# A two-layer network on one core: layer 0's attention hands ScalarE other tiles for its second squares, those of rows 4 to 6 of each head quad instead of rows 0 to 2

## The chip, the cores and the metric

The kernel runs on one core of a Trainium2 chip. Every time is device time in microseconds (us). The kernel before took 859.58 us as the median of 3 runs (859.4 to 862.9).

The engines carry these names in the profile: PE is TensorE's matmul part (PEld its weight load), DVE is VectorE, ACT is ScalarE, POOL is GpSimd. Each works through its own list of instructions strictly in order, and they meet at semaphores.

## The reference

Two layers, each an attention and a gated feed-forward part. The change is in layer 0's attention only: 1024 tokens, 16 heads of 16 channels, and a causal attention whose weights are not a softmax but the fourth power of the scores.

```python
def polynomial_attention(q, k, v, degree, is_causal):     # degree 4
    a = jnp.einsum('bhnd,bhmd->bhnm', q, k) ** degree
    if is_causal:
        a = jnp.tril(a)
    denom = jnp.sum(a, axis=-1, keepdims=True)
    return jnp.einsum('bhnm,bhmd->bhnd', a / denom, v)
...
xn = _layernorm(x)
s = _L0_attn_ref(xn, ...)            # changed stage
g = _silu(_L0_ffn_ref(xn, ...))
x = x + s * g                        # then layer 1
```

## The kernel before

Layer 0's attention stands between layer 0's feed-forward part and layer 1, and nothing of either runs beside it but a few small pieces. The 16 heads are worked in four **groups** of four heads. Inside a group a **row** is one block of 128 keys: row j (0 to 7) holds the scores of the keys 128j to 128j+127, on the partitions, against all queries from 128j on, so rows grow shorter, from 1024 queries down to 128. Rows are numbered through, R = 0 to 31, and R % 8 is j.

A row is cut into **units**, one PSUM bank pair each. In rows 0 to 3 a unit is two heads by half of the row's queries (four units per row); in rows 4 and 5 two heads by all queries (two units); rows 6 and 7 are one unit of four heads. That makes 22 units per group and 88 in all, of 1024, 896, 768, 640 or 512 elements per partition. Units 0 to 21 are the first group, 22 to 43 the second, 44 to 65 the third, 66 to 87 the fourth. In the second group units 22 to 25 are row 0, 26 to 29 row 1, 30 to 33 row 2, 34 to 37 row 3, 38 and 39 row 4, 40 and 41 row 5, 42 row 6, 43 row 7.

A unit goes through these steps:

- **scores** (PE, L595): the matmuls into one of three PSUM pairs. A pair is used again only when the first square of the unit that had it three steps earlier is done.
- **first square** (ACT, L1079): from PSUM into SBUF. Always ScalarE's.
- **second square** (in place in SBUF): on DVE (L1402, a tensor_tensor that multiplies the tile with itself) or, for units in ON_ACT0, on ACT (L1082). ScalarE takes the second square of unit n-1 after the first square of unit n.
- **mask** (POOL, L1772): an affine_select that zeroes the 128-wide diagonal block, only of the units that begin at a row's first query (u[2] == 0). 14 of a group's 22 units have one.
- **out** (PE, L613): the row's tile as the moving operand against the values, into two PSUM banks, one per half of the queries, when every second square and mask of the row is done.

Finished rows lie in a ring of four slots. Two of the slots reuse other tiles, so the trace calls row 0, 1, 4 and 5 of a group A, rows 2 and 6 qk_tok, and rows 3 and 7 stack. PE's order is a list worked out ahead (order0): a row's out comes behind the scores of the fourth unit after its last, one half at a time, with scores of the next unit between the halves. So out of row 2 of the second group stands just ahead of scores of unit 38.

At a group's end ACT copies the summed output out of PSUM (L1053, o_raw), PE transposes it (L624), and DVE divides (L1383 and L1385), which frees the PSUM pair of that transpose. The copy stands in ACT's list before the first square of the next group's unit 4, the division in DVE's list behind its unit 6. In the third group PE also transposes the divided output of the first two groups (L633), ACT rounds it (L1059, xT_hi) and DVE takes the rest (L1392, xT_lo), behind unit 55 in DVE's list.

Of the kernel before, what the change touches and what calls it, by code (L numbers as in the profile page):

```python
# [18 lines left out]
NT = TOK // P  # L19
# [16 lines left out]
def units0(j):  # L36

    w = (NT - j) * P
    size = 2 if j < 6 else 4
    cuts = [(0, w // 2), (w // 2, w)] if j < 4 else [(0, w)]  # L40
    return [(list(range(i, i + size)), a, e) for i in range(0, QUAD, size) for a, e in cuts]


UNITS0 = [(R, *unit) for R in range(ROWS0) for unit in units0(R % NT)]
DONE0 = [sum(1 for u in UNITS0 if u[0] <= R) for R in range(ROWS0)]
ON_ACT0 = [u[2] > 0 and u[1][0] == 2 and u[0] % NT < 3 for u in UNITS0]
BY_ACT0 = [sum(ON_ACT0[:n + 1]) for n in range(len(UNITS0))]
BY_DVE0 = [n + 1 - BY_ACT0[n] for n in range(len(UNITS0))]
MASKED0 = [sum(1 for u in UNITS0 if u[0] <= R and u[2] == 0) for R in range(ROWS0)]
# [105 lines left out]
def build_program(nc, x_in, wqkv_in, wout_in, lns_in, lnb_in, packed_in, scales_in,  # L155
# [5 lines left out]
    with ExitStack() as ctx:  # L161
        def sem(name):
            return ctx.enter_context(nc.semaphore(name))
# [94 lines left out]
        def A0_unit(n):  # L258

            R, heads, a, e = UNITS0[n]  # L260
            return A0_row(R)[:, heads[0]:heads[-1] + 1, a:e]
# [90 lines left out]
        def rows_of(b):  # L352
# [32 lines left out]
        s0_ps, s0_sq, s0_four, s0_four_act, s0_mask = (sem("s0_ps"), sem("s0_sq"), sem("s0_four"), sem("s0_four_act"),  # L385
                                               sem("s0_mask"))
# [126 lines left out]
        def _(pe):  # L513
# [300 lines left out]
            def logits(_, half):  # L814

                pe.wait_ge(rw_ready, 1)
                o = side_slot()
                tk = slice(half * HALF, (half + 1) * HALF)
                for c in range(NC):
                    last = mm3(o[0:NE, :], rw_hi[:, c], rw_lo[:, c], xT_hi[:, c, tk], xT_lo[:, c, tk], c == 0, c == NC - 1)  # L820
                last.then_inc(lgT_ps, 1)

            def turn_logits(*_):
                pe.wait_ge(lgT_copied, 2)
                o = side_slot()
                for t in range(NT):
                    last = pe.transpose(o[:, t * NE:(t + 1) * NE], lgT[:, t * P:(t + 1) * P], ident[0:NE, 0:NE])
                last.then_inc(lg_ps, 1)

            def ranks(*_):  # L830

                pe.wait_ge(mask_ready, 2)
                pe.wait_ge(rk_ready, 1)
                o = side_slot()
                chosen = r_m.rearrange("p t e -> p (t e)")
                pe.matmul(o[:, 0:NT * NE], before[:], chosen, start=True, stop=False)
                for t in range(1, NT):
                    pe.matmul(o[:, t * NE:NT * NE], ones[:], chosen[:, 0:(NT - t) * NE], start=False, stop=(t == NT - 1))
                for t in range(NT):
                    last = pe.matmul(o[:, NT * NE:(NT + 1) * NE], ones[:], r_m[:, t, :], start=(t == 0), stop=(t == NT - 1))  # L840
                last.then_inc(rk_ps, 1)
# [106 lines left out]
        def _(act):  # L948
# [115 lines left out]
            for n in range(len(UNITS0)):  # L1064
# [14 lines left out]
                act.activation(dst, src, ACT.Square).then_inc(s0_sq, 1)  # L1079
                if n >= 1 and ON_ACT0[n - 1]:  # L1080
                    act.wait_ge(s0_sq, n)
# [123 lines left out]
        def _(dve):  # L1205
# [191 lines left out]
            for n in range(len(UNITS0)):  # L1397
                R, heads = UNITS0[n][0:2]
                if not ON_ACT0[n]:
                    dve.wait_ge(s0_sq, n + 1)  # L1400
# [284 lines left out]
        def _(pool):  # L1685
# [81 lines left out]
            for n in range(len(UNITS0)):  # L1767
                if UNITS0[n][2]:
                    continue
                diag = A0_unit(n)[:, :, 0:P]  # L1770
                pool.wait_ge(s0_four, BY_DVE0[n])
                pool.affine_select(out=diag, in_=diag, compare_op=ALU.is_ge, fill=0.0, base=0,  # L1772
                                   pattern=[[0, len(UNITS0[n][1])], [1, P]], channel_multiplier=-1).then_inc(s0_mask, 1)
            def split_wqk(n):
# [251 lines left out]
```

## Time and profile before

| what | value |
|---|---|
| median of 3 runs | 859.58 us (859.4 to 862.9) |
| the profiled execution's own time | 856.94 us |
| its span, first to last instruction | 855.2 us |
| PE, DVE, ACT, POOL busy over the span | 92%, 71%, 54%, 50% |
| layer 0's attention, first square to last copy's start | 200.22 to 298.93 us of the span |
| in 199 to 300 us: PE, DVE, ACT, POOL busy | 78.8, 86.7, 84.8, 48.0 of 101 us |

The profiled execution is 2.6 us shorter than the median of the runs, so sums made in the trace are compared with 856.94 us and the difference is then added to 859.58. In the stage of the change no engine is busy throughout: what counts there is who waits for whom.

### The profile page before, as it was taken

What the parts mean: (1) busy time and instruction counts of PE and PEld (TensorE: products, weight loads), DVE (VectorE), ACT (ScalarE), POOL (GpSimd) and SP (SyncE); (2) the same over time, 40 slices, a digit from 0 to 9 for tenths busy, and PEclk for the clock granted to TensorE, in tenths of its full rate; (3) what the DMA queues carried; (4) which work ended last, traced back from release to release, by engine and by line L of the source; (5) the groups of instructions that cost most, each with busy time, mean ns of one, the idle gap of its engine ahead of it and who ended that gap; (6) DMA issues with size and microseconds to landing.
All of it is one profiled execution on the core that took longest, in us unless ns stands there. A gap on an engine that the chain in (4) does not pass through costs nothing.

```text
span 855.2 us, 13950 instructions
## 1 busy us (share of the span) xinstructions
PE 783.4 (92%) x4871; PEld 639.4 (75%) x4871; DVE 611.4 (71%) x1077; ACT 465.4 (54%) x822; POOL 423.7 (50%) x479
## 2 busy tenths in 40 slices
PE   6999999978777878898999999999999999999996
PEld 5776776754222367687988889989999999998884
DVE  8588868557998767888967886766767654445555
ACT  4433342279888733676645556565656555655431
POOL 1767837333555445445434447568663412665540
PEclk9999999998999989999999999999999999999999
DMA  5211194000000041000000001111110569643107
GB/s 182 75 38 37 38 292 135 1 1 1 1 1 1 1 126 30 22 7 11 21 8 13 8 25 57 38 38 49 47 44 1 207 126 351 214 149 106 51 5 243
DMA packets 50116, 59.82 MB, mean 70 GB/s; under 512 B 13559, under 2 KB 41084, under 8 KB 50048
## 3 DMA queue, kind: packets, MB, share of 16 engines
q1 hardware_dynamic: 45488, 50.49, 19.4%
q0 software_dynamic: 4560, 8.44, 2.8%
q8 instruction: 41, 0.67, 0.3%
q14 instruction: 27, 0.22, 0.1%
HBM read 41.11 MB, written 21.86 MB: 74 GB/s over the span
## 4 chain that ended last, share of the span: by engine, by line
PE 56%; DVE 12%; ACT 6%; POOL 6%; issue 5%; DMA 1%; POOLq 0%; ACTq 0%; DVEq 0%; SPq 0%
PE ps L786 12%; PE ps L516 8%; PE ps L518 8%; PE ps L517 8%; PE ps L879 4%; PE ps L876 3%; PE ps L910 3%; DVE cap L1477 2%; POOL A L1772 2%; DVE swap L1467 2%; PE ps L858 2%; PE ps L698 2%; PE ps L558 2%; PE ps L613 1%; PE ps L795 1%
## 5 line engine op out<-in xcount | busy, mean ns | idle before, releaser
L1131 ACT ACTIVATE cap<-cap 128x1024 f32<-128x1024 f32 (+7 forms) x128 | 87.1, 680 | 123.1 <-DVE cap L1477 123.0
L786 PE MATMUL ps<-V,P 128*128 128x129 f32 x1152 | 152.7, 279 | 0.0
L786 PEld LDWEIGHTS ps<-V,P 128*128 128x128 f32 x1152 | 145.3, 194 | 2.7
L1477 DVE SCALAR_TENSOR_TENSOR cap<-dist,ps 128x1024 f32<-128x1024 f32 (+7 forms) x128 | 95.1, 750 | 27.1 <-PE ps L518 22.1
L1696 POOL TENSOR_SCALAR_AFFINE_SELECT P<-P 128x128 f32<-128x128 f32 x128 | 38.8, 303 | 148.6 <-ACT P L1136 148.3
L1828 POOL DMA_INDIRECT y_scratch<-y_sb,aux_s x63 | 62.1, 985 | 61.2 <-ACT y_sb L1176 39.3
L1136 ACT ACTIVATE P<-cap 128x1024 f32<-128x1024 f32 (+7 forms) x128 | 87.6, 685 | 4.1
L516 PE MATMUL ps<-q_hi,k_hi 128*128 128x512 f32 x192 | 72.2, 376 | 7.9 <-DVE cap L1477 6.3
L518 PE MATMUL ps<-q_lo,k_hi 128*128 128x512 f32 x192 | 66.9, 349 | 0.0
L517 PE MATMUL ps<-q_hi,k_lo 128*128 128x512 f32 x192 | 66.8, 348 | 0.0
L1803 POOL TENSOR_TENSOR rot<-rot,swap 128x512 f32<-128x512 f32 x40 | 52.2, 1306 | 14.4 <-DVE swap L1467 14.2
L516 PE MATMUL ps<-xT_hi,w_hi 128*128 128x512 f32 x128 | 56.4, 441 | 2.9 <-POOL w_lo L1716 1.8
L1016 ACT ACTIVATE e_g<-ps 128x512 f32<-128x512 f32 x32 | 19.1, 598 | 68.5 <-PE ps L518 68.5
L1624 DVE TENSOR_SCALAR gu<-ps 128x256 f32<-128x256 f32 (+1 forms) x63 | 28.9, 459 | 38.0 <-PE ps L879 15.8
L1467 DVE TENSOR_TENSOR swap<-ps,sin 64x512 f32<-64x512 f32 x80 | 55.1, 688 | 1.1
L1402 DVE TENSOR_TENSOR A<-A 128x1024 f32<-128x1024 f32 (+2 forms) x40 | 49.6, 1287 | 4.4 <-ACT A L1079 4.4
L518 PE MATMUL ps<-xT_lo,w_hi 128*128 128x512 f32 x128 | 50.6, 396 | 0.0
L517 PE MATMUL ps<-xT_hi,w_lo 128*128 128x512 f32 x128 | 50.5, 394 | 0.0
L1168 ACT ACTIVATE sg<-gu 128x128 f32<-128x128 f32 (+1 forms) x63 | 20.4, 323 | 50.5 <-DVE gu L1624 50.5
L1079 ACT ACTIVATE A<-ps 128x1024 f32<-128x1024 f32 (+2 forms) x48 | 43.4, 965 | 7.7 <-PE ps L595 7.7
L595 PEld LDWEIGHTS ps<-QT,KT 64*128 64x128 f32 x192 | 16.4, 190 | 41.6 <-ACT A L1079 19.3
L516 PEld LDWEIGHTS ps<-q_hi,k_hi 128*128 128x128 f32 x192 | 36.6, 190 | 14.0 <-DVE cap L1477 7.8
(288 smaller groups left out, 2111.6 us busy)
## 6 DMA issues: line engine op xcount, KB each, us to landing
xg_scratch<-blank SPq DMA_DIRECT2D x1, 8127.0 KB, 31.2
xa<-xg_scratch SPq DMA_DIRECT2D x63, 128.0 KB, 2.3
ew<-in_experts SPq DMA_DIRECT2D x3, 1920.0 KB, 7.9
y<-y_scratch SPq DMA_DIRECT2D x8, 512.0 KB, 5.0
pk<-in_packed SPq DMA_DIRECT2D x8, 384.0 KB, 3.2
pks<-in_scales SPq DMA_DIRECT2D x8, 384.0 KB, 4.3
ew<-in_experts SPq DMA_DIRECT2D x1, 3072.0 KB, 11.2
wqk<-in_wqk SPq DMA_DIRECT2D x20, 128.0 KB, 2.0
```

The source lines that it names most:

```text
L516: pe.matmul(o, l_hi, r_hi, start=start, stop=False)
L517: pe.matmul(o, l_lo, r_hi, start=False, stop=False)
L518: return pe.matmul(o, l_hi, r_lo, start=False, stop=stop)
L786: last = pe.matmul(ps[:, 4 + r % 2, o:o + D1 + 1], P1[:, h % 2, a:a + P], V1[:, j, h // REP, :], start=(j == 0), stop=(j == t))
L1079: act.activation(dst, src, ACT.Square).then_inc(s0_sq, 1)
L1131: act.activation(cap[:, n % 2, 0:w], cap[:, n % 2, 0:w], ACT.Tanh, scale=1.0 / (CAP * float(D1) ** 0.5))\
L1136: act.activation(P1[:, h % 2, OFF[j]:OFF[j] + w], cap[:, n % 2, 0:w], ACT.Exp, scale=CAP)\
L1402: dve.tensor_tensor(a, a, a, ALU.mult).then_inc(s0_four, 1)
L1467: last = dve.tensor_tensor(swap[to, i % 2, :], b[frm, :], sin1[frm, tk], ALU.mult)
L1477: dve.scalar_tensor_tensor(out=cap[:, n % 2, 0:w], in0=dist[:, 0:w], scalar=slope, in1=psf[:, 1024 * (n % 2):1024 * (n % 2) + w], op0=ALU. ...
L1803: pool.tensor_tensor(r, r, swap[:, i % 2, :], ALU.add).then_inc(pj_rot, 1)
L1828: pool.indirect_dma_start(out=y_dram, out_offset=bass.IndirectOffsetOnAxis(ap=aux_s[:, b, 0:1].bitcast(U32), axis=0), in_=y_sb[:, b % YRIN ...
```

## The change

ON_ACT0, the list of units whose second square is ScalarE's, is another one. Before it held, in each group, the second head pair's second half of rows 0, 1 and 2 (units 3, 7 and 11 of the group; 1024, 896 and 768 elements; none of them masked). Now it holds the second head pair of rows 4 and 5 and the one unit of row 6 (units 17, 19 and 20 of the group; 1024, 768 and 1024 elements; all of them masked). So both before and after 3 of 22 squares per group are ScalarE's, and DVE has 19. The masks of the three units now wait for ScalarE's semaphore.

```diff
-ON_ACT0 = [u[2] > 0 and u[1][0] == 2 and u[0] % NT < 3 for u in UNITS0]
+ON_ACT0 = [(u[0] % NT in (4, 5) and u[1][0] == 2) or u[0] % NT == 6 for u in UNITS0]
 BY_ACT0 = [sum(ON_ACT0[:n + 1]) for n in range(len(UNITS0))]
 BY_DVE0 = [n + 1 - BY_ACT0[n] for n in range(len(UNITS0))]
...
                 diag = A0_unit(n)[:, :, 0:P]
-                pool.wait_ge(s0_four, BY_DVE0[n])
+                if ON_ACT0[n]:
+                    pool.wait_ge(s0_four_act, BY_ACT0[n])
+                else:
+                    pool.wait_ge(s0_four, BY_DVE0[n])
```

ACT's list before, from the first square of the second group's unit 26 on (the copy of the first group's output stands just ahead of it); 128x2x448 is a unit of row 1, 128x2x384 one of row 2 or row 5, by its tile:

```order
L1079 ACTIVATE A<-ps 128x2x448
L1082 ACTIVATE A<-A 128x2x512
L1079 ACTIVATE A<-ps 128x2x448 x3
L1079 ACTIVATE qk_tok<-ps 128x2x384
L1082 ACTIVATE A<-A 128x2x448
L1079 ACTIVATE qk_tok<-ps 128x2x384 x3
L1079 ACTIVATE stack<-ps 128x2x320
L1082 ACTIVATE qk_tok<-qk_tok 128x2x384
L1079 ACTIVATE stack<-ps 128x2x320 x3
L1079 ACTIVATE A<-ps 128x2x512 x2
L1079 ACTIVATE A<-ps 128x2x384 x2
L1079 ACTIVATE qk_tok<-ps 128x4x256
```

The same stretch of ACT's list after the change:

```order
L1079 ACTIVATE A<-ps 128x2x448 x4
L1079 ACTIVATE qk_tok<-ps 128x2x384 x4
L1079 ACTIVATE stack<-ps 128x2x320 x4
L1079 ACTIVATE A<-ps 128x2x512 x2
L1079 ACTIVATE A<-ps 128x2x384
L1082 ACTIVATE A<-A 128x2x512
L1079 ACTIVATE A<-ps 128x2x384
L1079 ACTIVATE qk_tok<-ps 128x4x256
L1082 ACTIVATE A<-A 128x2x384
L1079 ACTIVATE stack<-ps 128x4x128
L1082 ACTIVATE qk_tok<-qk_tok 128x4x256
L1079 ACTIVATE A<-ps 128x2x512 x4
```

The three second squares have left the first squares of rows 0 to 3 and stand among those of rows 4 to 7, all three ahead of the next group's first squares.

DVE's list before, from row 4 of the first group to row 3 of the second:

```order
L1402 TENSOR_TENSOR A<-A 128x2x512 x2
L1402 TENSOR_TENSOR A<-A 128x2x384 x2
L1402 TENSOR_TENSOR qk_tok<-qk_tok 128x4x256
L1402 TENSOR_TENSOR stack<-stack 128x4x128
L1402 TENSOR_TENSOR A<-A 128x2x512 x3
L1402 TENSOR_TENSOR A<-A 128x2x448 x3
L1383 RECIPROCAL o_rden<-ps 128x32
L1385 TENSOR_TENSOR xa<-ps,o_rden 128x8x64
L1402 TENSOR_TENSOR qk_tok<-qk_tok 128x2x384 x3
L1402 TENSOR_TENSOR stack<-stack 128x2x320 x4
```

And after:

```order
L1402 TENSOR_TENSOR A<-A 128x2x512
L1402 TENSOR_TENSOR A<-A 128x2x384
L1402 TENSOR_TENSOR stack<-stack 128x4x128
L1402 TENSOR_TENSOR A<-A 128x2x512 x4
L1402 TENSOR_TENSOR A<-A 128x2x448 x3
L1383 RECIPROCAL o_rden<-ps 128x32
L1385 TENSOR_TENSOR xa<-ps,o_rden 128x8x64
L1402 TENSOR_TENSOR A<-A 128x2x448
L1402 TENSOR_TENSOR qk_tok<-qk_tok 128x2x384 x4
L1402 TENSOR_TENSOR stack<-stack 128x2x320 x4
```

Three squares have left rows 4 to 6, and rows 0, 1 and 2 have four each instead of three; that of row 1 stands behind the division.

## Rows read from the trace of the kernel before

**Rows 1.** The page's first line.
```profile
span 855.2 us, 13950 instructions
```

**Rows 2.** Windows between chosen first squares: units 22, 44, 66, 83, last copy.
```profile
core 0: us, PE busy (x) PEld busy (x) DVE busy (x) ACT busy (x) POOL busy (x), PEclk, DMA share, GB/s
222.81:246.15 23.34, 18.28 (x154) 6.82 (x152) 21.49 (x22) 20.71 (x27) 12.17 (x15) 1.00 0.01 1
246.15:271.91 25.76, 20.73 (x162) 7.81 (x160) 22.63 (x24) 21.89 (x29) 12.16 (x15) 0.93 0.00 1
271.91:290.15 18.24, 15.43 (x116) 6.04 (x114) 15.79 (x17) 16.87 (x22) 7.51 (x11) 0.91 0.00 1
290.15:298.93 8.78, 5.74 (x60) 1.87 (x58) 7.07 (x7) 3.83 (x6) 7.01 (x7) 1.00 0.00 0
```

**Rows 3.** Timeline of ACT: start, length, line, tile, count, wait before.
```profile
228.65 1.07 ACT L1082 ACTIVATE A<-A 128x1024 f32<-128x1024 f32 x1
229.60 2.54 ACT L1079 ACTIVATE A<-ps 128x896 f32<-128x896 f32 x3
...
236.86 0.87 ACT L1082 ACTIVATE qk_tok<-qk_tok 128x768 f32<-128x768 f32 x1
...
240.35 1.02 ACT L1079 ACTIVATE A<-ps 128x1024 f32<-128x1024 f32 x1
241.28 1.51 ACT L1079 ACTIVATE A<-ps 128x768 f32<-128x768 f32 x2
...
246.15 1.94 ACT L1079 ACTIVATE A<-ps 128x1024 f32<-128x1024 f32 x2 [1.96 <-PE ps L595]
```

**Rows 4.** Timeline of DVE, first two groups.
```profile
201.38 3.70 DVE L1402 TENSOR_TENSOR A<-A 128x1024 f32<-128x1024 f32 x3 [1.92 <-ACT A L1079]
205.00 0.68 DVE L1407 TENSOR_TENSOR wout_lo<-wout,wout_hi 128x512 fp32r<-128x512 f32 x1
...
230.56 2.09 DVE L1402 TENSOR_TENSOR A<-A 128x896 f32<-128x896 f32 x2 [0.56 <-ACT A L1079]
232.57 0.35 DVE L1383 RECIPROCAL o_rden<-ps 128x32 f32<-128x32 f32 x1
232.96 0.69 DVE L1385 TENSOR_TENSOR xa<-ps,o_rden 128x512 f32<-128x512 f32 x1
...
235.03 1.83 DVE L1402 TENSOR_TENSOR qk_tok<-qk_tok 128x768 f32<-128x768 f32 x2 [0.52 <-ACT qk_tok L1079]
...
240.56 4.71 DVE L1402 TENSOR_TENSOR A<-A 128x1024 f32<-128x1024 f32 x4
...
246.54 0.89 DVE L1402 TENSOR_TENSOR stack<-stack 128x512 f32<-128x512 f32 x1
```

**Rows 5.** Timeline of POOL: the masks.
```profile
234.58 0.41 POOL L1772 TENSOR_SCALAR_AFFINE_SELECT qk_tok<-qk_tok 128x256 f32<-128x256 f32 x1 [1.45 <-DVE qk_tok L1402]
...
242.06 4.83 POOL L1772 TENSOR_SCALAR_AFFINE_SELECT A<-A 128x256 f32<-128x256 f32 x4 [1.14 <-DVE A L1402]
...
297.67 0.63 POOL L1772 TENSOR_SCALAR_AFFINE_SELECT stack<-stack 128x512 f32<-128x512 f32 x1
```

**Rows 6.** Timeline of PE: row passes, and scores of unit 57.
```profile
214.49 0.42 PE L613 MATMUL ps<-qk_tok,V 128*32 128x256 f32 x4 [0.36 <-ACT qk_tok L1082]
...
237.82 0.64 PE L613 MATMUL ps<-qk_tok,V 128*32 128x256 f32 x8 [0.36 <-ACT qk_tok L1082]
...
244.61 1.07 PE L613 MATMUL ps<-A,V 128*32 128x512 f32 x8 [1.31 <-POOL A L1772]
...
254.36 1.93 PE L613 MATMUL ps<-A,V 128*32 128x512 f32 x8
...
262.91 0.41 PE L595 MATMUL ps<-QT,KT 64*128 64x320 f32 x2 [0.59 <-DVE xT_lo L1392]
```

**Rows 7.** One line's own summary: shortest, median, longest in ns.
```profile
L1392 DVE TENSOR_TENSOR xT_lo<-ps,xT_hi x4: 681/691/692, 261.6 to 304.9; 128x512 fp32r<-128x512 f32 x4
```

**Rows 8.** Waits in 199 to 300 us: total, times, longest.
```profile
PE ps L613 <- POOL A L1772: 8.7, 8, 1.4
```

## The prediction

> **What bounds the kernel now.** I read the windows first, then the timeline of each engine in the second group, the one group in which TensorE had its full clock throughout. The span is 855.2 us of an execution that took 856.94 [rows 1]. The windows run from the first square of unit 22 to that of unit 44 (the second group, 23.34 us), on to unit 66 (25.76), to unit 83 (18.24) and to the last copy (8.78) [rows 2]. In the second group ACT is busy 20.71 us and DVE 21.49 of 23.34: neither is full, so the order of waits sets the time, and I follow it in two parts.
>
> The **head** is rows 0 to 3, up to the first square of unit 39. There ACT has first and second squares in one queue, and PE's pass over row 2 (L613, 237.82) waits 0.36 us for ACT's second square of unit 33, which ends at 236.86 + 0.87 = 237.73 [rows 3, 6]. So ACT bounds the head. In the **tail**, rows 4 to 7, DVE runs four squares from 240.56 on without a gap, and the masks queue behind them: four masks take 4.83 us, where one alone takes 0.41 [rows 4, 5]. PE waits 1.31 us for a mask at 244.61, the scores behind that pass come late, and ACT sits idle 1.96 us before 246.15 [rows 3, 6]. The tail is bound by DVE and masks, the head by ACT. The change moves ACT's help from the one to the other; what it brings is what the tail can still use, less what the head now lacks.
>
> **What one square costs.** On DVE, call a the start-to-start time of a 1024 square, and m what a mask adds that slips in between two squares. The three from 201.38 to 205.00 hold one mask: 3a + m = 3.62. Those from 240.56 to 245.20 (4.71 long, less the 0.08 by which a 3.70 row outlasts its 3.62) are two of 1024 and two of 768 with three masks, 4.64. A 768 square is (1.83 - 0.07) / 2 = 0.88, an 896 square (232.57 - 230.56) / 2 = 1.005 [rows 4]. So 2a + 3m = 2.88, which gives a = 1.14, m = 0.20. A mask that waits is done 0.35 us after the next square has started: the four end at 246.89, and the square started at 246.54 [rows 4, 5]. The division is 0.99 (232.57 to 233.65, less the overlap).
>
> Behind that stands a rule: the Trainium skill, SBUF — State Buffer, section "SBUF: two separate sides", says that VectorE and GpSimd share one pair of SBUF ports as an exclusive lock, held for a whole instruction, against a VectorE operation with two SBUF inputs. The masks agree: 0.41 alone, some 1.2 beside back-to-back squares. By the rule alone, squares on ScalarE free the masks, and the change would be a gain; that is a rival below.
>
> On ACT a second square of 1024 is 0.95 (228.65 to 229.60), 0.12 less than its length, so one of 768 is 0.87 - 0.12 = 0.75. A first square is (1.94 - 0.10) / 2 = 0.92 for 1024 and (1.51 - 0.10) / 2 = 0.70 for 768, so about 0.48 for 512 [rows 3].
>
> **The tail after the change.** From the first square of unit 39, ACT's list holds 39, 40, second 39, 41, 42, second 41, 43, second 42, and then unit 44: 0.92 + 0.70 + 0.95 + 0.70 + 0.92 + 0.75 + 0.48 + 0.95 = 6.37 us. Before it was 246.15 - 240.35 = 5.80 with the idle time in it [rows 3]. ACT has no gap there any more: the idle 1.96 us are filled with 2.65 us of squares, and unit 44 comes 0.57 later. The passes over rows 4 to 7 wait for ACT's squares instead of masks and stay ahead of it. DVE, freed of 1.14 + 0.88 + 1.14 + 0.60 for masks, is idle before unit 44, which gains nothing, since its work comes from ACT.
>
> **The head after the change.** Now DVE has four squares of each of rows 0, 1 and 2. It can't start them before ACT has made the first one, so I count from ACT's first square of unit 44. That one is done 1.02 later; but ACT's second square of unit 42 ends 0.12 after unit 44's first square starts, so the masks of 42 and 43 run from 0.17 on, 0.63 each with DVE idle [rows 5], and DVE starts behind them at 1.43. Then 4 x 1.14 + 4 x 1.005 + 4 x 0.88 + 0.99 for the division = 13.09, and four masks slip in (rows 0, 0, 1 and 2; the others fall in gaps or the division), 0.80: the square of unit 55 ends at 15.32. The mask of unit 54 ends 0.35 behind and PE starts 0.10 after it: 15.77. Before, the same pass came at 237.82 - 222.81 = 15.01 [rows 2, 6]. The head becomes DVE's, 0.76 longer. From that pass to the first square of the next row 4's second unit it is 240.35 - 237.82 = 2.53 both times.
>
> What is queued behind this pass: scores of unit 38 and on (PE is in order), so all of ACT's tail. The two parts don't overlap, for each begins with what the other ends with.
>
> **The sum.**
> - Second group: 0.76 + 0.57 = +1.33.
> - First group: no lead. 201.38 + 4 x 1.14 + 0.61 (L1407) + 4 x 1.005 + 4 x 0.88 = 214.09, with five masks 215.09, and + 0.45 = 215.54, against 214.49 [rows 4, 6]: +1.05, and +0.57 for its tail: +1.62.
> - Third group: DVE ends unit 55 at 15.32, then two of L1392 at 0.69 [rows 7] = 16.70, when scores of unit 57 may start; before they started at 262.91 - 246.15 = 16.76, after the same instruction [rows 6]. Head -0.06, tail +0.57: +0.51.
> - Fourth group: 15.77 + 2.53 = 18.30 against 18.24 [rows 2]: +0.06. This and the third group lost time before to the half clock (granted 0.93 and 0.91): eight matmuls took 1.93 us at 254.36 and 1.07 at 244.61 [rows 2, 6]. It fell early in the head, where the new head has slack on PE. At the very end no group follows: ACT's last second square ends 6.37 + 0.12 later, two masks alone 1.26 + 0.05, then 0.63 to the copy as before (298.93 - 298.30): 8.43 against 8.78: -0.35. Together -0.29.
>
> Sum +1.33 + 1.62 + 0.51 - 0.29 = **+3.2 us**: 856.94 becomes 860.1 in the profiled execution, and the median 859.58 becomes **862.8**. Nothing else is priced: PE's instructions stay, the masks' other semaphore costs a wait on either engine, 0 by its kind; the work behind the stage waits for its end and shifts whole.
>
> **The rivals.**
> - *The head keeps up.* The mask costs and the late start are the least sure terms. Without them DVE's chain ends at 1.06 + 13.09 + 0.45 = 14.6, under 15.01, and only the tail's 0.57 stays: 3 x 0.57 + 0.05 - 0.35 = +1.4, 861.0. For it: masks are not always in the way; against it: DVE would be full 13 us on end. 17%.
> - *Masks are freed (faster).* PE waited 8.7 us in the stage for masks of tile A [rows 8]. If these waits go and the next rows come earlier by as much: 859.6 - 8.7 = 850.9. It decides if ACT's tail comes out under 5.80 us and the head doesn't wait for DVE. Against it: 6.37 of instructions stand in ACT's list, and nothing can go round it. 15%. The rule of the Trainium skill's page SBUF — State Buffer, told above, speaks for this one.
> - *Half clock in the wrong place (slower).* PE now waits longer in the head, right before the pass over row 2 and the stretch of 2.53 us in which PE is the chain. If the clock falls to half there, a pass costs 1.93 for 1.07 and the smaller one and the scores some 0.35 more, 1.2 a group: in three groups +3.6, 866.4. For it: two of the three windows before had such a stretch. 18%.
> - Forecast as summed: 50%, its own range 860.5 to 866.
>
> **How the numbers follow.** No change within 0.5% (4.3 us) is about what a measurement of this kernel can't tell from nothing. The forecast lies at +3.2, inside it for 33 of its 50 points and over it for 17; with the head that keeps up 17 more, so 33 + 17 = 0.50 for the same. Slower: 17 + 18 = 0.35. Faster 0.15. Range: the upper end takes in the half clock, 868; the lower stops short of freed masks, but takes in a half of their gain against the head's loss, 857. Outside lie some 10% below and 8% above.
>
> **What would show it.** Right: DVE squares of rows 0 to 2 in an unbroken run of about 13 us in each group, PE's pass over row 2 waiting for DVE or its mask at about 15.8 us after the first square of the group; ACT with gaps in the head and none in the tail; masks of rows 4 to 6 at 0.4 to 0.8 instead of 1.1; from unit 22 to 44 some 24.7 us. Wrong: ACT still idle before unit 44, or that window under 23.3; or a stage of equal length with the difference elsewhere; or a granted clock in the stage far under 0.93.

## The result, and the profile after

The changed kernel took 862.07 us (median of 20 runs, 858.73 to 868.38), the kernel before 859.49 beside it: ratio 1.0033, 95% interval 1.0017 to 1.0049, so 1.5 to 4.2 us slower, 2.8 in the middle (the medians differ by 2.6). The predicted 862.8 was 3.2 over the 859.58 of before.

The windows of the changed kernel, cut at the same squares as [rows 2] (first squares of units 22, 44, 66, 83 and the last copy):

```profile
core 0: us, PE busy (x) PEld busy (x) DVE busy (x) ACT busy (x) POOL busy (x), PEclk, DMA share, GB/s
223.53:248.00 24.47, 19.88 (x156) 7.08 (x152) 20.43 (x21) 20.91 (x28) 11.77 (x14) 0.93 0.01 1
248.00:273.95 25.95, 21.18 (x164) 8.06 (x160) 21.52 (x23) 21.80 (x29) 10.60 (x14) 0.93 0.00 1
273.95:292.11 18.16, 13.33 (x112) 5.26 (x108) 17.04 (x18) 14.60 (x20) 8.82 (x10) 1.00 0.00 1
```

The second group is 24.47 us against 23.34, the third 25.95 against 25.76, the fourth up to unit 83 18.16 against 18.24.

ACT's timeline in the second group (start, length, line, tile, count, and in brackets the idle time ahead):

```profile
228.06 3.67 ACT L1079 ACTIVATE A<-ps 128x896 f32<-128x896 f32 x4
233.30 0.81 ACT L1079 ACTIVATE qk_tok<-ps 128x768 f32<-128x768 f32 x1 [1.57 <-PE ps L595]
234.95 2.21 ACT L1079 ACTIVATE qk_tok<-ps 128x768 f32<-128x768 f32 x3 [0.83 <-PE ps L595]
...
241.69 1.73 ACT L1079 ACTIVATE A<-ps 128x1024 f32<-128x1024 f32 x2 [0.40 <-PE ps L595]
243.30 1.06 ACT L1082 ACTIVATE A<-A 128x1024 f32<-128x1024 f32 x1
...
247.05 1.09 ACT L1082 ACTIVATE qk_tok<-qk_tok 128x1024 f32<-128x1024 f32 x1
248.00 3.80 ACT L1079 ACTIVATE A<-ps 128x1024 f32<-128x1024 f32 x4
```

The gaps have changed sides. Before, ACT was idle 1.96 us at the end of the tail [rows 3]; now it has gaps in the head and none from 241.69 to the next group's first square at 248.00: 6.31 us, against 5.80.

DVE, POOL and PE in the same head:

```profile
224.62 8.45 DVE L1402 TENSOR_TENSOR A<-A 128x1024 f32<-128x1024 f32 x7 [1.17 <-ACT A L1079]
233.00 0.34 DVE L1383 RECIPROCAL o_rden<-ps 128x32 f32<-128x32 f32 x1
...
233.98 1.08 DVE L1402 TENSOR_TENSOR A<-A 128x896 f32<-128x896 f32 x1
234.98 3.76 DVE L1402 TENSOR_TENSOR qk_tok<-qk_tok 128x768 f32<-128x768 f32 x4
```
```profile
237.94 1.07 POOL L1775 TENSOR_SCALAR_AFFINE_SELECT qk_tok<-qk_tok 128x256 f32<-128x256 f32 x1 [0.88 <-DVE qk_tok L1402]
...
246.77 0.41 POOL L1775 TENSOR_SCALAR_AFFINE_SELECT A<-A 128x256 f32<-128x256 f32 x1 [1.38 <-ACT A L1082]
```
```profile
239.15 0.64 PE L613 MATMUL ps<-qk_tok,V 128*32 128x256 f32 x8 [0.93 <-POOL qk_tok L1775]
```

DVE starts 1.09 us after ACT's first square and works without a gap to 238.74. PE's pass over row 2 waits 0.93 us for the mask at 237.94, which ends at 239.01, behind the last of these squares, where in [rows 6] it waited 0.36 for ACT. It comes 239.15 - 223.53 = 15.62 us after the group's first square, against 15.01. A mask behind one of ACT's squares in the tail (246.77) takes 0.41, as in [rows 5] a mask alone does; that gains nothing there, since ACT's list is what ends last.

### The profile page after: what moved, and what is told of

Read it like the earlier page. It is cut to its first block, busy times and chain, and to the rows that moved or that the text cites. A ratio compares the mean times of both kernels' runs of the same rounds, so it can differ in the third digit from the quotient of the medians.

```text
span 859.8 us, 13950 instructions
## 1 busy us (share of the span) xinstructions
PE 789.2 (92%) x4871; PEld 643.5 (75%) x4871; DVE 605.7 (70%) x1077; ACT 466.1 (54%) x822; POOL 422.3 (49%) x479
## 4 chain that ended last, share of the span: by engine, by line
PE 54%; DVE 17%; issue 6%; ACT 5%; POOL 3%; DMA 1%; POOLq 0%; ACTq 0%; DVEq 0%; SPq 0%
PE ps L786 12%; PE ps L516 8%; PE ps L518 8%; PE ps L517 8%; DVE A L1402 4%; PE ps L879 4%; PE ps L876 3%; PE ps L910 3%; DVE cap L1477 2%; DVE swap L1467 2%; PE ps L558 2%; PE ps L698 2%; PE ps L858 1%; DVE qk_tok L1402 1%; PE ps L795 1%
## 5 line engine op out<-in xcount | busy, mean ns | idle before, releaser
L1806 POOL TENSOR_TENSOR rot<-rot,swap 128x512 f32<-128x512 f32 x40 | 52.2, 1305 | 14.5 <-DVE swap L1467 14.3
L1402 DVE TENSOR_TENSOR A<-A 128x1024 f32<-128x1024 f32 (+2 forms) x40 | 47.4, 1232 | 5.6 <-ACT A L1079 5.4
L1814 POOL TENSOR_TENSOR q_lo<-rot,q_hi 128x512 fp32r<-128x512 f32 x32 | 41.3, 1290 | 9.7 <-ACT q_hi L1125 9.5
```

The costliest lines, as they stand in the source:

```text
L1402: dve.tensor_tensor(a, a, a, ALU.mult).then_inc(s0_four, 1)
L1806: pool.tensor_tensor(r, r, swap[:, i % 2, :], ALU.add).then_inc(pj_rot, 1)
L1814: pool.tensor_tensor(lo[:, hd % 2, tk], rot[:, k % 3], hi[:, hd % 2, tk].bitcast(F32), ALU.subtract)\
```

## The experiments

All are edits of ON_ACT0 in the changed kernel, but for the small masks and the repeats. "Head set" is what ScalarE had before, units 3, 7 and 11 of a group; "both sets" adds the changed kernel's 17, 19 and 20. "Head" below is from a group's first square to PE's pass over its row 2, "tail" from the first square of the group's unit 17 (unit 39 in the second group) to the next group's first square (for the fourth, to the last copy). Between them lie 2.53 to 2.55 us in every group of the thirteen profiles but one. From the start times in the traces, with the stage from first square to last copy's start:

| kernel | heads of the four groups | tails | stage | ratio (95%) |
|---|---|---|---|---|
| before | 14.27, 15.01, 17.40, 15.71 | 5.79, 5.79, 5.81, 8.78 | 98.71 | 1 |
| before, again | 14.77, 16.17, 16.26, 15.88 | 5.79, 5.80, 5.82, 8.78 | 99.40 | |
| changed | 15.33, 15.62, 17.10, 15.62 | 6.31 three times, 8.37 | 101.11 | 1.0033 (1.0017 to 1.0049) |
| changed, again | 15.52, 16.49, 17.10, 15.62 | 6.31 three times, 8.36 | 102.15 | |
| no square on ACT | 15.52, 16.40, 17.88, 16.40 | 5.91, 5.91, 5.10, 9.63 | 104.41 | 1.0035 (1.0011 to 1.006) |
| both sets | 15.00, 16.47, 18.47, 16.71 | 6.31 three times, 8.37 | 104.09 | 1.0012 (0.9985 to 1.0039) |
| both sets, again | 15.00, 15.20, 16.21, 15.72 | 6.31 three times, 8.36 | 99.56 | |
| small masks | 14.38, 15.24, 16.84, 16.52 | 6.31 three times, 7.83 | 99.87 | 1.0011 (0.9984 to 1.0038) |
| head set and unit 17 | 15.05, 15.19, 17.69, 15.18 | 4.88, 4.86, 4.89, 8.06 | 95.94 | 0.9969 (0.9938 to 1.0) |
| the same, again | 15.01, 15.91, 16.43, 15.19 | 4.86, 4.89, 4.89, 8.58 | 95.92 | 0.9945 (0.9922 to 0.9967) |
| head set and unit 19 | 14.76, 15.95, 17.11, 15.45 | 5.79, 5.79, 5.81, 8.05 | 98.86 | 0.997 (0.9943 to 0.9997) |
| units 3, 7 and 17 | 15.32, 15.47, 17.73, 15.50 | 5.03, 5.02, 4.89, 8.16 | 97.27 | 0.9982 (0.996 to 1.0004) |
| units 3, 7, 11, 17, 19 | 15.01, 15.40, 15.96, 14.70 | 5.36, 5.37, 5.37, 8.57 | 95.89 | 0.995 (0.9926 to 0.9973) |

**No second square on ScalarE.**

```diff
-ON_ACT0 = [(u[0] % NT in (4, 5) and u[1][0] == 2) or u[0] % NT == 6 for u in UNITS0]
+ON_ACT0 = [False for u in UNITS0]
```

> No second square on ScalarE at all. Theory (two parts in line: a head, rows 0 to 3, that waits for whoever squares last, and a tail, rows 4 to 7, that ends where ScalarE reaches the next group's first square): the head is DVE's as in the changed kernel and starts later, the tail is that of the kernel before. From the first square of a group to the pass over its row 2: 16.4 us in the second group (before 15.01, changed 15.62), because DVE starts 1.2 after the first square and two masks of 512 add 0.43 each. From the first square of unit 39 to that of unit 44: 5.8 (before 5.80, changed 6.31). Stage sum about +3.8 us against before, ratio 1.0044. Rival A (only the tail's list on ScalarE costs): this kernel equals the one before, 1.000 or less. Rival B (balance of totals: DVE with 22 squares is the bound, its 21.5 us of a 23.3 us group grow by 3): second group some 25.5 us, evenly late in head and tail.

Measured: 861.04 us against 857.98, 1.0035. Its DVE, PE and ACT in the second group:

```profile
224.24 9.11 DVE L1402 TENSOR_TENSOR A<-A 128x1024 f32<-128x1024 f32 x7
...
239.44 0.64 PE L613 MATMUL ps<-qk_tok,V 128*32 128x256 f32 x8 [1.21 <-POOL qk_tok L1775]
```
```profile
247.89 1.03 ACT L1079 ACTIVATE A<-ps 128x1024 f32<-128x1024 f32 x1 [2.07 <-PE ps L595]
```

Seven squares take 9.11 us, 1.44 more than where the masks are small (7.67, below): two masks of 512 and three of 256 have slipped in, 2 x 0.43 + 3 x 0.20 = 1.46. The pass comes 16.40 us after the first square at 223.04, where 16.4 was expected, and ACT is idle 2.07 us in the tail, about as before (1.96). So the head gets longer without any square on ACT in the tail: the loss isn't the tail's list alone, and the group isn't late evenly (tail 5.91).

The stage of this profile is 5.7 and 5.0 us longer than in the two of before, more than the expected 3.8. In its third group 4.06 us lie between head and tail instead of 2.5:

```profile
265.77 0.89 PE L613 MATMUL ps<-qk_tok,V 128*32 128x256 f32 x8
266.59 0.80 PE L595 MATMUL ps<-QT,KT 64*128 64x512 f32 x2
267.31 1.93 PE L613 MATMUL ps<-qk_tok,V 128*32 128x512 f32 x8
```

The granted clock over 265 to 268.6 us was 0.64, and the pass over row 2 took 0.89 and 1.93 us for the usual 0.64 and 1.06. In no other profile was the stretch behind the head lengthened.

**Both sets on ScalarE.**

```diff
-ON_ACT0 = [(u[0] % NT in (4, 5) and u[1][0] == 2) or u[0] % NT == 6 for u in UNITS0]
+ON_ACT0 = [(u[2] > 0 and u[1][0] == 2 and u[0] % NT < 3) or (u[0] % NT in (4, 5) and u[1][0] == 2) or u[0] % NT == 6 for u in UNITS0]
```

> ScalarE takes both sets, units 3, 7, 11 and 17, 19, 20 of each group. Theory: head as before (pass over row 2 at 15.0 us after the group's first square), tail as in the changed kernel (6.31 us from unit 39 to unit 44); stage about +1.1 us against before, ratio 1.0013. Rival A (only the tail costs): stage as in the changed kernel, +2.4, 1.0028. Rival B (totals: ScalarE with 28 of its own instructions is the bound at 20.7 + 2.7 = 23.4 of 23.3 us): ScalarE without gaps in the head as well and a second group of 23.4 to 24.

Measured: ratio 1.0012, near the expected 1.0013, though its interval (0.9985 to 1.0039) doesn't exclude rival A's 1.0028. Its profile agreed in the tail, 6.31, and not in the head, 16.47 instead of 15.0. PE in that head:

```profile
228.61 1.94 PE L624 MATMUL ps<-ident,o_raw 128*128 128x128 f32 x8 [1.34 <-ACT A L1079]
...
231.15 1.93 PE L613 MATMUL ps<-A,V 128*32 128x512 f32 x8
...
233.63 1.73 PE L613 MATMUL ps<-A,V 128*32 128x512 f32 x8
```

Three times eight matmuls that take 1.06 to 1.07 at full clock took 1.94, 1.93 and 1.73: TensorE ran at half clock, 1.2 GHz, for most of this stretch (granted 0.54 over 228 to 235.5 us), and all four heads had such a stretch (granted 0.71 to 0.84 over a whole head). So the kernel was profiled once more.

> The kernel with both sets on ScalarE once more, for another profile. In its first profile a group's head took 16.47 us instead of the expected 15.0, with TensorE at half clock for 6.8 us in every head. Theory: the head is 15.0 to 15.3 wherever the clock is full, and longer by the matmuls' own lengthening where it is half, some 0.9 for each eight matmuls of 512 on the chain. Rival: 16.5 whatever the clock.

Measured: 15.00 and 15.20 in the first two groups, 16.21 in the third (17.40 and 16.26 in the two profiles of before), the tail 6.31 again, 859.86 us. So the rival's 16.5 whatever the clock falls. No head of this profile had full clock throughout (granted 0.71 to 0.91), yet the stage came to 99.56, 0.85 over before's first profile and 0.16 over its second, where the sum of a head as before and a longer tail has 1.1.

**The kernels before and after, profiled once more.** Since half clock moves between executions, both got a second profile.

> The kernel before once more, for another profile. Theory: head 15.0 in a group with full clock throughout, up to 1.5 more where half clock covers matmuls of the head (before, the second group had none); the tail from unit 39 to unit 44 is 5.8 in every group. Rival: head and tail both move by half a microsecond from execution to execution, and the differences between kernels are of that size.

> The changed kernel once more, for another profile. Theory: its head is VectorE's run of squares, which half clock in the early head doesn't touch: 15.6 +- 0.1 in the second and fourth group again wherever half clock falls before the pass over row 2, tail 6.31. Rival: the head follows the clock, 15.0 to 16.5.

Measured, before again (857.75 us): the second group's head is 16.17 instead of 15.01, with a granted clock of 0.66 over 229 to 234 us, so half clock for most of it:

```profile
230.73 1.93 PE L613 MATMUL ps<-A,V 128*32 128x512 f32 x8
...
233.21 1.35 PE L613 MATMUL ps<-A,V 128*32 128x512 f32 x8
...
238.61 0.64 PE L613 MATMUL ps<-qk_tok,V 128*32 128x256 f32 x8 [0.36 <-ACT qk_tok L1082]
```

The tail is 5.80, as before. The changed kernel's first profile had such a stretch in the same microseconds (0.57 over 230 to 234), and its head was 15.62, by 0.55 the shorter one. In the changed kernel again (863.88 us) half clock lasted twice as long there, and the head was 16.49. The window and DVE in it:

```profile
229.00:236.00 7.00, 5.94 (x28) 2.54 (x28) 6.90 (x8) 4.26 (x6) 2.94 (x3) 0.51 0.00 0
```
```profile
236.04 0.96 DVE L1402 TENSOR_TENSOR qk_tok<-qk_tok 128x768 f32<-128x768 f32 x1
237.78 2.70 DVE L1402 TENSOR_TENSOR qk_tok<-qk_tok 128x768 f32<-128x768 f32 x3 [0.78 <-ACT qk_tok L1079]
```

With the clock granted at 0.51 over 7 us, DVE's run does break, 0.78 us at 237.78, because the scores behind the slow passes come late. So the run of squares covers a short stretch at half clock and not a long one. The expectation of 15.6 wherever it falls was wrong for this group; there the rival's 15.0 to 16.5 held. In the fourth group, at full clock in both profiles of the changed kernel, the head was 15.62 both times.

**Small masks.**

```diff
-                diag = A0_unit(n)[:, :, 0:P]
+                diag = A0_unit(n)[:, :, 0:16]
...
-                                   pattern=[[0, len(UNITS0[n][1])], [1, P]], channel_multiplier=-1).then_inc(s0_mask, 1)
+                                   pattern=[[0, len(UNITS0[n][1])], [1, 16]], channel_multiplier=-1).then_inc(s0_mask, 1)
```

> The changed kernel with masks of 16 instead of 128 columns per head (most of the causal zeroing of the diagonal blocks is left out), so the same instructions and waits at an eighth of the work. Theory: in the head a mask between two squares adds 0.20 us, five of them up to the pass over row 2 add 0.97, and the mask after the last square 0.35: with small masks the pass comes at about 14.5 us after the group's first square instead of 15.62; the tail is ScalarE's list and stays at 6.2 to 6.3. Stage some 3.5 us under the changed kernel, ratio to before 0.999. Rival A (masks wait for a port but cost DVE nothing that matters; ScalarE bounds the stage): 15.5, ratio 1.003. Rival C (the masks bound the tail too): tail under 5.8 as well, ratio under 0.997.

Measured: 859.92 against 857.98, ratio 1.0011. By the ratios that is 1.9 us under the changed kernel and not 3.5, and the two intervals overlap; the stage is 1.2 and 2.3 us under those of the changed kernel's two profiles. DVE and POOL, second and first group:

```profile
223.62 7.67 DVE L1402 TENSOR_TENSOR A<-A 128x1024 f32<-128x1024 f32 x7 [1.17 <-ACT A L1079]
```
```profile
204.05 1.14 POOL L1775 TENSOR_SCALAR_AFFINE_SELECT A<-A 128x32 f32<-128x32 f32 x1 [1.14 <-DVE A L1402]
```

Seven squares take 7.67 us where they took 8.45 with full masks: 0.78 for four masks, 0.20 each, the price in the prediction. And a mask of an eighth of the work still takes 1.14 beside DVE's squares: its length is the square it waits behind, not its own work. In the same trace such a mask takes 1.01 behind a square of 896, 0.87 behind one of 768 and 0.74 behind one of 640, each the start-to-start time of that square.

This is the exclusive lock that the Trainium skill, SBUF — State Buffer, section "SBUF: two separate sides", describes for a VectorE operation with two SBUF inputs against a GpSimd operation that reads SBUF: whichever starts first has the shared ports for its whole instruction, and the other is blocked. POOL's side agrees with it; on DVE's side the trace has a loss of 0.20 us, less than the 0.41 that the mask takes alone.

The first group's head came down by 0.95, near the expected 1.1. In the second it came down only 0.38 (15.24, nearer to rival A's 15.5 than to 14.5) and the tail by nothing: with DVE's run shorter, the passes at half clock (1.93 and 1.53 for eight) and the scores behind them are the next bound, which I had left out. The fourth group's head was even longer, 16.52 for 15.62, with a granted clock of 0.82 in it, where the changed kernel had 1.00.

**One square for the tail, unit 17.** The head set stays on ACT as before.

```diff
-ON_ACT0 = [(u[0] % NT in (4, 5) and u[1][0] == 2) or u[0] % NT == 6 for u in UNITS0]
+ON_ACT0 = [(u[2] > 0 and u[1][0] == 2 and u[0] % NT < 3) or (u[0] % NT == 4 and u[1][0] == 2) for u in UNITS0]
```

> ScalarE keeps units 3, 7, 11 of each group as before and takes unit 17 (row 4, second pair) as well. Theory: the head stays 15.0; in the tail ScalarE fills part of the 1.96 us in which it was idle, the mask of unit 39 is done by 243.5 instead of 244.5 on the clock of the trace before, the pass over row 4 and with it the first square of unit 44 come 0.95 earlier, so 4.85 us from unit 39 to unit 44 instead of 5.80. Stage -3.5 to -4, ratio 0.9954. Rival A (any second square on ScalarE in the tail costs its own 0.95): tail 5.8 to 6.7, ratio 1.000 to 1.004. Rival B (the tail is bound by the chain of masks of all units up to row 7): gain under 0.3 a group, ratio 0.999.

> Units 3, 7, 11 and 17 once more, timed anew. Theory: tail 4.87 again, head 15.1 to 15.3, ratio 0.996 to 0.998 with an interval that, with that of the first run, excludes 1. Rival (the first ratio of 0.9969 was chance): 0.999 to 1.001.

Measured: tails of 4.86 to 4.89 in the first three groups of both profiles (expected 4.85). The ratio was 0.9969 (0.9938 to 1.0; expected 0.9954) and then 0.9945 (0.9922 to 0.9967; expected 0.996 to 0.998), 853.98 us against 859.31. The stage is 2.8 us shorter than in before's first profile, both times, where 3.5 to 4 was expected; in the second profile the second group's head was 15.91, at a granted clock of 0.91, and not 15.1 to 15.3. ACT, POOL and PE, second profile:

```profile
242.83 1.06 ACT L1082 ACTIVATE A<-A 128x1024 f32<-128x1024 f32 x1
...
246.11 1.02 ACT L1079 ACTIVATE A<-ps 128x1024 f32<-128x1024 f32 x1
```
```profile
243.96 0.81 POOL L1775 TENSOR_SCALAR_AFFINE_SELECT A<-A 128x256 f32<-128x256 f32 x2 [0.63 <-ACT A L1082]
```
```profile
244.55 1.06 PE L613 MATMUL ps<-A,V 128*32 128x512 f32 x8 [0.38 <-POOL A L1775]
```

The square of unit 39 is done on ACT while ACT would have waited, its mask and the next take 0.81 together, and PE's wait ahead of the pass over row 4 is 0.38 in place of 1.31 [rows 6].

**Unit 19 instead of unit 17.** The same edit with row 5 for row 4.

> ScalarE keeps units 3, 7, 11 and takes unit 19 (row 5) instead of unit 17 of the run before. Theory (the next group's first square hangs on the pass over row 4, so on the masks of units 38 and 39, not on how much of ScalarE's idle time is filled): from unit 39 to unit 44 stays 5.8 (before 5.80; 4.87 with unit 17), ratio 1.000, at best 0.999. Rival (what helps is any square taken off VectorE in the tail): 5.8 - 0.75 = 5.05, ratio 0.997.

```profile
245.01 1.07 PE L613 MATMUL ps<-A,V 128*32 128x512 f32 x8 [1.31 <-POOL A L1775]
```
```profile
246.55 1.94 ACT L1079 ACTIVATE A<-ps 128x1024 f32<-128x1024 f32 x2 [1.23 <-PE ps L595]
```

The tail stays at 5.79: PE waits 1.31 us for the mask as before, and 0.73 of ACT's idle time is filled for nothing. So what counts here is which square is taken. The timed ratio was 0.997 (0.9943 to 0.9997), below the expected 1.000, at best 0.999, and it is the rival's number; but the rival's tail of 5.05 did not come. The last tail is 0.73 shorter, which accounts for 0.999, and the rest is within the interval.

**Units 3, 7 and 17, and units 3, 7, 11, 17 and 19.** The conditions `u[0] % NT < 2` with row 4, and `u[0] % NT < 3` with rows 4 and 5.

> ScalarE has units 3, 7 and 17: three of 22 squares, as many as before and in the changed kernel. Theory: the tail is 4.9 from unit 39 to unit 44 as with units 3, 7, 11, 17; in the head VectorE has 11 squares up to row 2 in place of 10 and gaps enough for one more, so the pass over row 2 comes at 15.2 to 15.4 after the group's first square (15.19 there). Ratio 0.997. Rival (the head needs all three on ScalarE, and each one given to VectorE costs its 0.88 to 1.14): pass at 16, ratio 1.000.

> ScalarE has units 3, 7, 11, 17 and 19. Theory: from unit 39 to unit 44 ScalarE's list holds 0.92 + 0.70 + 0.95 + 0.70 + 0.92 + 0.75 + 0.48 = 5.42 without a gap, so 5.4: between 4.87 (unit 17 alone) and 5.80 (before). Ratio 0.998. Rival (the tail is masks and VectorE): 4.6 to 4.9 with less work on VectorE, ratio 0.996 or less.

Measured: three units, as many as before and after the change, give 0.9982 (0.996 to 1.0004) with tails of 4.89 to 5.03 and a second head of 15.47, a little over the expected 15.2 to 15.4; the ratio's interval holds both the expected 0.997 and the rival's 1.000. Five units give tails of 5.37 (expected 5.4) and 853.53 us, ratio 0.995 (0.9926 to 0.9973), better than the expected 0.998 by more than the tail explains; its heads of 15.96 and 14.70 in the last two groups are the shortest seen there, in one profile. Its ACT at the end of the tail:

```profile
245.12 0.86 ACT L1082 ACTIVATE A<-A 128x768 f32<-128x768 f32 x1
245.86 0.62 ACT L1079 ACTIVATE stack<-ps 128x512 f32<-128x512 f32 x1
246.33 3.94 ACT L1079 ACTIVATE A<-ps 128x1024 f32<-128x1024 f32 x4
```

No gap, so the rival (4.6 to 4.9) falls. The kernel with units 3, 7, 11 and 17 (in its second timing) and the one with unit 19 added are faster than the kernel before, and their intervals lie clear of the changed kernel's too; between themselves the intervals don't decide.

Part of their gain goes with TensorE's clock. In the second timing the six executions with units 3, 7, 11 and 17 had granted clocks of 0.979 to 0.988 over the whole kernel, those of before 0.970 to 0.982. The executions between 0.979 and 0.982 alone have medians of 854.45 and 857.37, 2.9 us apart, which is what the stage shows (2.8); whether the set itself brings the higher clock isn't shown.

## Why the prediction was right

**The tail, +0.57 a group.** It was +0.51: 6.31 in all fifteen tails, of five profiles, that have this set on ACT and a group behind them, with small masks and with the head set added too. ACT's list of eight instructions was the right thing to add up.

**The head, +0.76.** +0.61 between the first two profiles of the second group. One term of the working was wrong in its form: DVE did not wait for the masks of units 42 and 43 to end, it started 1.09 after the first square and not 1.43. The mask of unit 43 was still running (224.33 to 224.97) and made DVE's first square 0.20 longer, as the others did theirs. Five times 0.20 and a lead of 1.09 make 15.6; four and 1.43 made 15.77, so two errors partly cancel. Nor is the +0.61 taken at equal clocks: the second group's head had full clock throughout before and a granted 0.91 after. In before's second profile that head had 0.91 too and took 16.17, longer than the changed kernel's 15.62. The loss of 0.6 thus stands against a head of before at full clock.

**The sum of the groups.** Forecast +1.62, +1.33, +0.51, -0.29 for the first group to the fourth. The first profiles differ by +1.58, +1.13, +0.19 and -0.49, together +2.4; the second ones by +1.28, +0.83, +1.32 and -0.68, together +2.8 (102.15 - 99.40). The timed difference is +2.8 by the ratio, +2.6 by the medians. The middle two groups move with the half clock, which lengthened one kernel's head or the other's. The third group's -0.06 for the head rests on that: the changed kernel's 17.10 came both times, close to the working (scores of unit 57 at 16.46 for 16.70), but the 17.40 it was compared with held half clock (granted 0.91). In before's second profile that head had full clock and took 16.26, so the same mechanism costs 0.84 there. That the four groups add up to within a microsecond of the forecast is in part luck: the third group's difference was +0.19 in the first pair of profiles and +1.32 in the second. That the fourth group would gain at the end because no mask is left beside DVE's squares was right: 8.37 against 8.78, forecast 8.43.

**The rivals.** That the head keeps up: it did not, PE waits for the mask behind DVE's last square (0.93 us). Freed masks: they were freed, 0.41 for 1.1 to 1.4, and PE's wait for masks of tile A before row 4 fell from 1.31 to 0.44, but ACT's list took over the end. The relief paid with unit 17 alone (tail 4.87) or with 17 and 19 (5.37). Half clock in the wrong place: in the place that this rival names, the pass over row 2 and the 2.53 us behind it, it never fell in a profile of the changed kernel; the kernel with no square on ACT shows what it costs there, 4.06 for 2.53. Half clock earlier in the head did lengthen it, by 0.9 us in the changed kernel's second profile (16.49 against 15.62) and 1.3 in both sets' first (16.47 against 15.20), and the kernel before by 1.2. What share the timed medians hold isn't shown.

**What stays open.** The first profiled executions differ by 4.6 us in the span, of which 2.4 lie in the stage and -0.9 ahead of it; 3.1 lie behind it, and the second profiles differ there by 2.7. Behind the stage the instructions are the same, and the eleven further profiles have 553.5 to 560.0 us there. The three profiles with the changed set of units (small masks included) have 559.4 to 560.0, at the upper end; but two profiles of one kernel, both sets, have 554.0 and 558.5. As the timed medians differ by 2.6 in all, I take the difference behind the stage as chance, but it isn't shown. A large part of the spread goes with TensorE's clock: the changed kernel's five executions with a granted clock of 0.980 or more took 858.7 to 862.4 us, the four with 0.972 or less 866.0 to 868.4.

## What to carry to other kernels

Where two engines share out like work, their busy totals don't show which should take a piece. Find the instruction that waits in each stretch, and give away the piece whose end it waits for, as long as the taker's own list still ends in time for its next fixed duty. Here one square of the right unit was worth 0.9 us a group, one of the wrong unit nothing, and three cost 0.5. Idle time of an engine in one stretch doesn't pay for work taken away in another: the help that was taken from the head cost 0.6 us there in the second group, and the tail could not use all of it.

## What the runs showed of the hardware

A mask on POOL beside back-to-back squares on DVE, each with two SBUF inputs, costs DVE little and POOL about the whole square. DVE loses 0.20 us for a mask of 256 elements and next to nothing for one of 32. That 0.20 is also how much longer a mask of 256 takes alone than one of 32, 0.41 against 0.21. For 512 elements DVE loses 0.43, from three squares of the kernel before with two such masks and one of 256 beside them: 4.56 - 0.08 = 4.48, less 3 x 1.14 and 0.20, halved.

```profile
224.02 4.56 DVE L1402 TENSOR_TENSOR A<-A 128x1024 f32<-128x1024 f32 x3
```

POOL takes 1.06 to 1.39 us for 256 elements beside squares of 768 to 1024, and still 1.14 for 32 behind one of 1024. I had not expected that so small an operation would take that long.

TensorE's half clock came in stretches at other places in each execution of the same kernel: before had none in the second group in one profile and one at about 230 to 234 us in the other, which made its head 16.17 instead of 15.01. Comparing single profiles of one group can thus be off by more than the change itself. The tails with a group behind them had the full clock in all thirteen profiles and repeated to 0.03 us where a kernel was profiled twice. The last tail did not: with units 3, 7, 11 and 17 it was 8.06 at full clock and 8.58 at a granted 0.86.
